# Weighted sums with the support stationary: one float32r matmul in place of four bf16 matmuls in a two-layer graph kernel

## The chip, the cores and the metric

The kernel runs on one core of a Trainium2 chip. The metric is the device time of one execution in microseconds (us); lower is better. The engines are TensorE (PE; its weight loads are PEld), VectorE (DVE), ScalarE (ACT), GpSimd (POOL) and SyncE (SP), which here issues nearly all DMAs. SBUF is the core's memory, PSUM the one that TensorE writes to.

## The reference

Two graph layers with residuals over 2048 nodes of 64 features; `adj` is a sparse 2048 x 2048 matrix of zeros and ones.

```python
# layer 0
support = x @ weight
mask = (adj != 0)
rank = cumsum(mask, axis=1); deg = rank[:, -1:]
k = minimum(deg, 100.0)
pos = rank - (deg - k)
w = mask * where(pos > 0, 0.5 ** (k - pos), 0.0)
x = layernorm(x + w @ support + bias)
# layer 1
deg = clip(sum(adj, axis=1, keepdims=True) + 1, 1, None)
h = (adj @ x + x) / deg
z = relu(concatenate([x, h], axis=1) @ W + b)
x = layernorm(x + z / maximum(norm(z), 1e-12))
```

The weight of an edge is a power of two whose exponent is the number of ones to its right in its row.

## The kernel before, in words

The rows of `adj` (2048) stand in four quarters q = 0..3 of 512 rows, its columns in 16 blocks b of 128. It is loaded in 16 units of 1 MB (`stage`, a ring of 8), one for a quarter and four column blocks. SP issues all loads in a fixed order, u0 to u15. A unit is turned so that columns stand on partitions (`adjT`): TensorE transposes it in two groups of eight 128 x 128 pieces into a bank of `tmp` (L837) and DVE copies that out (L533). The last four units (u12 to u15) are turned by DMA instead: DVE packs such a unit to bf16 in four casts (`pack`, L488), and SP issues a DMA transpose (L239).

Layer 0 runs as two chains, c = 0 (quarters 0, then 2) and c = 1 (quarters 1, then 3), each 32 steps long, from the last column block to the first. Step n of a chain does three things.

- `count`: two 512-column matmuls (L856 with `rest`, L858 with `suffix`) add to a PSUM bank `cnt[:, c]` so that it holds, for every edge of this block, the bit pattern of its power of two.
- `weights` (ACT, L324): a Relu that writes these as int16, which read as bf16 are the weights `wts`. The next `count` of this chain adds to the same bank and waits for it, so that a chain can't step faster than one round trip PE - ACT - PE.
- `weigh`: for each 128 of the 512 rows a matmul with the weights stationary and `sup` moving (L869, four of 192 columns) adds to `acc`. `sup` is the support in three bf16 parts, side by side.

A hand-written loop over ticks orders all engines. In tick t TensorE does `count(0, t)`, `weigh(0, t - 3)`, what belongs to index m = t + 2 (transposes of a group of `adj`, x1T, yu), `count(1, t - 5)` and `weigh(1, t - 8)`. DVE runs over the same m in its own order: parts of `finish_layer0`, the copy of the group, then `pack` where PACKS says so (m = 21 to 24). Every queue is in order, so what DVE has in front of a copy holds the `count` that reads it.

`finish_layer0(q, part)` turns the sums of a quarter into `x1`: part 0 adds the three parts of the sum (a reduction from `acc`, L455), part 1 adds `xs` (L458), part 2 takes statistics (L438), part 3 centres (L464), part 4 scales (four small operations L443 to L447, then L469). x1 is transposed (L879) and multiplied by W (L888, "yu"), and parts 6 and 7 split the result into three bf16 parts `ysp`. Layer 1's aggregation (L900) and its elementwise end follow.

Of the kernel before, what the change touches and what calls it, by code (L numbers as in the profile page):

```python
# [44 lines left out]
F32 = mybir.dt.float32  # L45
BF16 = mybir.dt.bfloat16
# [3 lines left out]
def build(nc, x, adj, w0, b0, w1, b1, out):  # L50
    with ExitStack() as ctx:
# [25 lines left out]
        ident32 = sb("ident32", [P, P], F32)  # L77
        wd0 = sb("wd0", [P, 2, D], F32)
# [22 lines left out]

        agg = [acc[:, 0:RT, :], cnt[:, :, :].rearrange("p b (h n) -> p (b h) n", h=2), acc[:, RT:2 * RT, :],
# [8 lines left out]
        wd_zeroed = sem("wd_zeroed")  # L111
        zeroed = sem("zeroed")
# [8 lines left out]
        sup_left = sem("sup_left")  # L121
        sup_mid = sem("sup_mid")
# [4 lines left out]
        w_ready = [sem(f"w_ready{i}") for i in range(2)]  # L127
        w_used = [sem(f"w_used{i}") for i in range(2)]
# [46 lines left out]
        for m in range(TICKS):  # L175
# [11 lines left out]
        fills += [("x1T", 2), ("yu", 2), ("x1T", 3), ("yu", 3)]  # L187
# [59 lines left out]
        def _(pool):  # L247
# [18 lines left out]
            select(rest, ALU.not_equal, -float(EXP1 * (NEIGH + 1))).then_inc(consts, 1)  # L266
            nc.gpsimd.memset(power[:, :], -0.5).then_inc(power_set, 1)
# [754 lines left out]
```

## Time and profile before

| | |
|---|---|
| median of 3 runs | 111.45 us (111.05 to 112.16) |
| the profiled execution | 110.99 us, of which the span from first to last instruction is 109.2 us |
| busy: PE, PEld, DVE, ACT, POOL | 91.9, 73.7, 61.3, 58.0, 18.8 us |
| chain that ended last | PE 72%, DVE 13%, DMA 4%, ACT 4% |
| mean granted TensorE clock | 0.975 |

Times are counted from the first instruction. A row of the groups gives busy time and the mean of one instruction, which for a matmul holds its latency: back to back they start much closer. What a matmul costs in a stream is read from the chain that ended last, where its row holds only the time by which it moved the chain. The rows of a DMA's issue and of its landing are in two views: landing is counted from the start of the issue.

### The profile page before, as it was taken

The numbers are of one execution on the slowest core, as the hardware profiler recorded it, in microseconds if no ns is written. First come the engines' busy times: TensorE is split into PE (matmuls) and PEld (weight loads), VectorE is DVE, ScalarE is ACT, GpSimd is POOL, SyncE is SP. The second block draws the span as 40 slices with busy tenths as digits, with TensorE's granted clock in tenths as the row PEclk, the third lists the DMA queues.
The fourth block names the chain that finished last, engine by engine and source line by source line (L and its number), as shares of the span: only waits on it lengthen the run. The fifth ranks groups of instructions, "written<-read, shape, count | busy, mean of one in ns | idle before, by whom it ended". The sixth has DMA issues, their size and how long they took to land.

```text
span 109.2 us, 2379 instructions
## 1 busy us (share of the span) xinstructions
PE 91.9 (84%) x876; PEld 73.7 (67%) x876; DVE 61.3 (56%) x186; ACT 58.0 (53%) x126; POOL 18.8 (17%) x44
## 2 busy tenths in 40 slices
PE   0349299999999999999999999999999999996000
PEld 0248068777777777777676676678988999995000
DVE  1003527564525247899998402226378339999991
ACT  0602644396665656666648886633214208479640
POOL 6200000000000142200074200000000000367870
PEclk9999999999999999999999999999999999999955
DMA  2999999799999999999799910000000000000224
GB/s 61 297 300 349 373 388 369 252 393 388 385 388 388 384 389 385 386 378 202 169 213 212 115 28 0 6 0 0 0 6 0 0 0 0 6 0 0 48 53 94
DMA packets 22314, 20.23 MB, mean 185 GB/s; under 512 B 13600, under 2 KB 14624, under 8 KB 22304
## 3 DMA queue, kind: packets, MB, share of 16 engines
q1 hardware_dynamic: 22144, 20.06, 61.2%
q8 instruction: 7, 0.11, 0.4%
q10 hardware_dynamic: 160, 0.03, 0.1%
q14 instruction: 3, 0.02, 0.1%
HBM read 17.47 MB, written 0.52 MB: 165 GB/s over the span
## 4 chain that ended last, share of the span: by engine, by line
PE 72%; DVE 13%; DMA 4%; ACT 4%; issue 3%; SPq 1%; DVEq 0%
PE acc L869 18%; PE cnt L856 13%; PE cnt L858 12%; PE tmp L837 10%; PE acc L900 7%; PE cnt L900 5%; DMA stage<-in_adj_dram 4%; PE tmp L888 3%; DVE stats L438 3%; DVE t L571 3%; ACT wts L324 2%; PE acc L914 2%; DVE t L582 1%; PE tmp L879 1%; PE tmp L914 1%
## 5 line engine op out<-in xcount | busy, mean ns | idle before, releaser
L324 ACT ACTIVATE wts<-cnt 128x512 int16<-128x512 f32 x64 | 37.8, 597 | 23.1 <-PE cnt L858 22.8
L869 PEld LDWEIGHTS acc<-sup,wts 128*128 128x128 bf16 x256 | 22.9, 98 | 13.5
L869 PE MATMUL acc<-sup,wts 128*128 128x192 bf16 x256 | 31.2, 246 | 0.0
L533 DVE COPY adjT<-tmp 128x1024 bf16<-128x1024 bf16 x24 | 16.5, 688 | 20.9 <-PE tmp L837 20.9
L856 PE MATMUL cnt<-adjT,rest 128*128 128x512 bf16 x60 | 22.8, 380 | 2.3 <-ACT wts L324 2.2
L858 PE MATMUL cnt<-adjT,suffix 128*128 128x512 bf16 x64 | 24.5, 383 | 0.0
L837 PE MATMUL tmp<-ident,stage 128*128 128x128 bf16 x192 | 15.5, 227 | 1.9 <-DMA stage<-in_adj_dram 1.9
L275 POOL TENSOR_TENSOR adjT<-adjT,ident 128x128 bf16<-128x128 bf16 x16 | 7.3, 487 | 49.9 <-PE cnt L858 49.9
L837 PEld LDWEIGHTS tmp<-ident,stage 128*128 128x128 bf16 x192 | 13.1, 102 | 3.0 <-issue 2.5
L900 PE MATMUL acc<-ysp,adjT 128*128 128x194 bf16 x128 | 12.4, 247 | 0.0
L900 PEld LDWEIGHTS acc<-ysp,adjT 128*128 128x128 bf16 x128 | 11.0, 98 | 0.2
L279 POOL TENSOR_TENSOR small<-square,power 128x4 f32<-128x4 f32 (+1 forms) x4 | 4.2, 1056 | 34.5 <-DVE square L603 34.5
L856 PEld LDWEIGHTS cnt<-adjT,rest 128*128 128x128 bf16 x60 | 5.8, 97 | 4.5 <-ACT wts L324 3.7
L374 ACT ACTIVATE u<-u,degree 128x64 f32<-128x64 f32 x16 | 4.4, 337 | 4.9 <-DVE degree L567 4.8
L455 DVE TENSOR_REDUCE t<-acc 128x256 f32<-128x768 f32 x4 | 3.8, 954 | 5.4 <-PE acc L869 5.4
L858 PEld LDWEIGHTS cnt<-adjT,suffix 128*128 128x128 bf16 x64 | 6.3, 99 | 0.4
L900 PE MATMUL cnt<-ysp,adjT 128*128 128x194 bf16 x64 | 6.4, 247 | 0.0
L474 DVE TENSOR_TENSOR left<-tmp,ysp 128x256 f32<-128x256 f32 x4 | 1.7, 419 | 7.5 <-ACT ysp L335 7.5
L438 DVE BATCH_NORM_STATS2 stats<-t 128x6 f32<-128x128 f32 x23 | 5.7, 285 | 0.1
L488 DVE CAST nat<-stage 128x512 bf16<-128x512 f32 x16 | 5.7, 417 | 0.0
L900 PEld LDWEIGHTS cnt<-ysp,adjT 128*128 128x128 bf16 x64 | 5.5, 98 | 0.2
L900 PE MATMUL tmp<-ysp,adjT 128*128 128x194 bf16 x64 | 5.6, 247 | 0.0
(98 smaller groups left out, 83.8 us busy)
## 6 DMA issues: line engine op xcount, KB each, us to landing
stage<-in_adj_dram SPq DMA_DIRECT2D x15, 1024.0 KB, 14.0
stage<-in_adj_dram SPq DMA_DIRECT2D x4, 256.0 KB, 4.4
xs<-in_x_dram SPq DMA_DIRECT2D x2, 256.0 KB, 5.7
out_dram<-xs SPq DMA_DIRECT2D x3, 128.0 KB, 2.0
out_dram<-xs SPq DMA_DIRECT2D x2, 64.0 KB, 1.7
wd<-in_L_gnn_W_dram SPq DMA_DIRECT2D x4, 16.0 KB, 8.3
adjT<-nat SPq DMA_TRANSPOSE x4, 5.4
wd<-in_L_gnn_weight_dram ACTq DMA_DIRECT2D x2, 16.0 KB, 4.0
```

The lines of the kernel that those rows point to most:

```text
L275: nc.gpsimd.tensor_tensor(d, d, ident16[:, :], ALU.add).then_inc(diag_ready, 1)
L279: nc.gpsimd.tensor_tensor(small[:, 3, batch(k)], square[:, batch(k)], power[:, 0:size(k)], ALU.pow).then_inc(norm_ready[k], 1)
L324: nc.scalar.activation(wts[:, c, n % WRING, :].bitcast(I16), cnt[:, c, :], ACT.Relu).then_inc(w_ready[c], 1)
L374: nc.scalar.activation(u1[:, t, :], u1[:, t, :], ACT.Copy, scale=degree[:, t:t + 1]).then_inc(weighted[k], 1)
L438: yield nc.vector.bn_stats(stats[:, k, t:t + 2, :].rearrange("p s c -> p (s c)"), data[:, t:t + 2, :].rearrange("p t d -> p d t"))
L488: nc.vector.tensor_copy(nat[:, i, r, :], stage[:, u % RING, r, :]).then_inc(nat_ready, 1)
L533: nc.vector.tensor_copy(adjT[:, q, bp // 2, :, bp % 2 * 2:bp % 2 * 2 + 2, :], bank.bitcast(BF16).rearrange("p (r k n) -> p r k n", r=RT, k ...
L837: last = nc.tensor.transpose(bank[:, (2 * r + k) * P:(2 * r + k + 1) * P], halves[:, r, 2 * j0 + 1:2 * (j0 + P):2], ident16[:, :])
L856: nc.tensor.matmul(cnt[:, c, :], rest[:, :], block_of(q, b + 1), start=False, stop=False, skip_group_check=True)
L858: nc.tensor.matmul(cnt[:, c, :], suffix[:, :], block_of(q, b), start=(b == NB - 1), stop=True, skip_group_check=True).then_inc(cnt_done[c], 1)
L869: last = nc.tensor.matmul(acc[:, c * RT + r, 0:PD], wts[:, c, n % WRING, r * P:(r + 1) * P], sup[:, b, :], start=(b == NB - 1 and r % 2 == ...
L900: last = nc.tensor.matmul(agg[g][:, r, 0:PD + 2], adjT[:, g, b // QB, r, b % QB, :], ysp[:, b, 0:PD + 2], start=first, stop=(b == NB - 1), ...
```

## The change

`weigh` becomes one matmul: `sup` (128 columns, now two float32r parts of 64) is stationary, the 512 weights of the step stream past it as float32r, and the result is the transposed sum [128 = 2 parts x 64, 512 rows] in one bank `accT[q]`. ACT writes the weights as before, now to `w16`; a new POOL copy (`widen`) makes float32r of them. When a quarter ends, ACT copies the bank to SBUF (`copy_sums`) and TensorE multiplies each 128 rows of it by `fold`, two stacked identities (`fold_sums`, four float32 matmuls of 64 columns), which transposes back and adds the parts. Part 0 on DVE goes; parts 1 to 7 and what follows them come one or two ticks later. The split of the support needs one DVE operation where it needed two and an ACT copy.

In the head, ten matmuls on zeros (`warm`) stand before and after the first transposes, DVE and no longer ACT copies the first xT, and `ORDER` swaps m = 5 and 6. The operations on the diagonal (POOL, L275) are placed in the tick loop. The casts of `pack` stay at m = 21 to 24.

```diff
-WHEN = {0: (0, 1, 2), 1: (3,), 2: (4,), 6: (6,), 7: (7,)}
-WRING = 4
+WHEN = {2: (1, 2), 3: (3,), 4: (4,), 7: (6,), 8: (7,)}
+WRING = 3
+SRING = 2
+ORDER = (0, 1, 2, 3, 4, 6, 5) + tuple(range(7, TICKS))
+WARM = (6, 4)
+DIAG_AT = (16, 18, 25, 27)
+COPIED = (NB - 1 + LAG, NB - 1 + LAG + BEHIND, STEPS - 1 + LAG)
...
+            def widen(c, n):
+                pool.wait_ge(w_ready[c], n + 1)
+                if n >= WRING:
+                    pool.wait_ge(w_used[c], n - WRING + 1)
+                nc.gpsimd.tensor_copy(wts[:, c, n % WRING, :], w16[:, c, n % SRING, :]).then_inc(w_cast[c], 1)
...
+            def copy_sums(q):
+                act.wait_ge(w_used[q % 2], (q // 2 + 1) * NB)
+                if q >= 2:
+                    act.wait_ge(tmp_full, number[("sum", q - 1)] + 1)
+                nc.scalar.copy(sums[:, min(q, 1), :], accT[q]).then_inc(acc_read, 1)
...
-                if part == 0:
-                    dve.wait_ge(w_used[c], (q // 2 + 1) * NB)
-                    sums = acc[:, c * RT:(c + 1) * RT, 0:PD].rearrange("p t (k d) -> p t d k", k=PARTS)
-                    nc.vector.reduce_sum(t0[:, v, :], sums, AX_X).then_inc(acc_read, 1)
...
-                for r in range(RT):
-                    last = nc.tensor.matmul(acc[:, c * RT + r, 0:PD], wts[:, c, n % WRING, r * P:(r + 1) * P],
-                                            sup[:, b, :], start=(b == NB - 1 and r % 2 == 0), stop=(b == 0),
-                                            skip_group_check=True)
-                last.then_inc(w_used[c], 1)
+                nc.tensor.matmul(accT[q], sup[:, b, :], wts[:, c, n % WRING, :], start=(b == NB - 1), stop=(b == 0),
+                                 skip_group_check=True).then_inc(w_used[c], 1)
+
+            def fold_sums(q):
+                bank = tmp_bank(("sum", q))
+                pe.wait_ge(acc_read, q + 1)
                 for r in range(RT):
+                    last = nc.tensor.matmul(bank[:, r * D:(r + 1) * D], sums[:, min(q, 1), r * P:(r + 1) * P], fold[:, :],
+                                            start=True, stop=True)
+                last.then_inc(tmp_full, 1)
```

TensorE's row around ticks 24 to 26, before: first the transposes of x1 of quarter 0, then count(1, 18) and so on; the third pair of counts is count(1, 19), behind the transposes of group m = 26.

```order
L879 MATMUL tmp<-ident,x 128x128 x2
L856 MATMUL cnt<-adjT,rest 128x512
L858 MATMUL cnt<-adjT,suffix 128x512
L869 MATMUL acc<-sup,wts 128x192 x4
L856 MATMUL cnt<-adjT,rest 128x512
L858 MATMUL cnt<-adjT,suffix 128x512
L869 MATMUL acc<-sup,wts 128x192 x4
L888 MATMUL tmp<-wd,x1T 128x256 x2
L837 MATMUL tmp<-ident,stage 128x128 x8
L856 MATMUL cnt<-adjT,rest 128x512
L858 MATMUL cnt<-adjT,suffix 128x512
L869 MATMUL acc<-sup,wts 128x192 x4
```

The same stretch now, from count(0, 24); L860 are the transposes of `adj`, L879 and L881 `count`, L889 `weigh`, L905 x1T, L914 yu.

```order
L879 MATMUL cnt<-adjT,rest 128x512
L881 MATMUL cnt<-adjT,suffix 128x512
L889 MATMUL acc<-wts,sup 128x512
L905 MATMUL tmp<-ident,x 128x128 x2
L860 MATMUL tmp<-ident,stage 128x128 x8
L879 MATMUL cnt<-adjT,rest 128x512
L881 MATMUL cnt<-adjT,suffix 128x512
L889 MATMUL acc<-wts,sup 128x512
L879 MATMUL cnt<-adjT,rest 128x512
L881 MATMUL cnt<-adjT,suffix 128x512
L889 MATMUL acc<-wts,sup 128x512
L914 MATMUL tmp<-wd,x1T 128x256 x2
```

Four matmuls have become one, and x1T and yu of the quarter each stand one tick later.

DVE's row from the first pack (m = 21) to the copy of the group m = 24 and the last pack, before (L443 to L469 are part 4).

```order
L488 CAST nat<-stage 128x512 x4
L443 RECIPROCAL small<-root 128x4
L444 SCALAR_TENSOR_TENSOR small<-small 128x4
L445 SCALAR_TENSOR_TENSOR small<-stats,small 128x4
L447 SCALAR_TENSOR_TENSOR small<-small 128x4
L469 TENSOR_TENSOR x<-t,small 128x256
L533 COPY adjT<-tmp 128x4x256
L488 CAST nat<-stage 128x512 x4
L533 COPY adjT<-tmp 128x4x256
L488 CAST nat<-stage 128x512 x4
L533 COPY adjT<-tmp 128x4x256
L488 CAST nat<-stage 128x512 x4
```

And now, from the second pack (m = 22) to the copy of the group m = 26 (L517 is the cast of a pack, L557 the copy of a group).

```order
L517 CAST nat<-stage 128x512 x4
L493 SCALAR_TENSOR_TENSOR t<-stats,t 128x256
L557 COPY adjT<-tmp 128x4x256
L517 CAST nat<-stage 128x512 x4
L475 RECIPROCAL small<-root 128x4
L476 SCALAR_TENSOR_TENSOR small<-small 128x4
L477 SCALAR_TENSOR_TENSOR small<-stats,small 128x4
L479 SCALAR_TENSOR_TENSOR small<-small 128x4
L498 TENSOR_TENSOR x<-t,small 128x256
L557 COPY adjT<-tmp 128x4x256
L517 CAST nat<-stage 128x512 x4
L557 COPY adjT<-tmp 128x4x256
```

Part 4 now stands between the third pack and the copy of the group m = 24, where nothing stood.

TensorE's row at the end of chain 1, before: the last three `weigh` with aggregation (L900) between them, then x1T and yu of quarter 2.

```order
L900 MATMUL acc<-ysp,adjT 128x194 x8
L869 MATMUL acc<-sup,wts 128x192 x4
L900 MATMUL acc<-ysp,adjT 128x194 x8
L869 MATMUL acc<-sup,wts 128x192 x4
L900 MATMUL acc<-ysp,adjT 128x194 x8
L869 MATMUL acc<-sup,wts 128x192 x4
L879 MATMUL tmp<-ident,x 128x128 x2
L900 MATMUL cnt<-ysp,adjT 128x194 x8
L888 MATMUL tmp<-wd,x1T 128x256 x2
```

And now (L926 is aggregation, L896 `fold_sums`).

```order
L926 MATMUL acc<-ysp,adjT 128x194 x8
L896 MATMUL tmp<-fold,u 128x64 x4
L889 MATMUL acc<-wts,sup 128x512
L926 MATMUL acc<-ysp,adjT 128x194 x8
L889 MATMUL acc<-wts,sup 128x512
L926 MATMUL acc<-ysp,adjT 128x194 x8
L889 MATMUL acc<-wts,sup 128x512
L905 MATMUL tmp<-ident,x 128x128 x2
L926 MATMUL cnt<-ysp,adjT 128x194 x8
L896 MATMUL tmp<-fold,u 128x64 x4
L914 MATMUL tmp<-wd,x1T 128x256 x2
```

The sum of quarter 2, which DVE took when chain 0 had ended, is now made on TensorE, three `weigh` and two aggregations ahead of x1T.

## Rows read from the trace of the kernel before

**Rows 1.** The page: the span in 40 slices of 2.73 us

```profile
PE   0349299999999999999999999999999999996000
...
DVE  1003527564525247899998402226378339999991
...
PEclk9999999999999999999999999999999999999955
...
GB/s 61 297 300 349 373 388 369 252 393 388 385 388 388 384 389 385 386 378 202 169 213 212 115 28 0 6 0 0 0 6 0 0 0 0 6 0 0 48 53 94
```

**Rows 2.** The chain that ended last: start us, us moved; one full tick

```profile
32.28 0.45 PE tmp L837 x8
32.73 0.22 PE cnt L856
...
33.16 0.33 PE acc L869 x4
...
34.25 0.45 PE tmp L837 x8
```

**Rows 3.** The same chain: the head, and float32 matmuls later

```profile
6.93 1.01 PE tmp L837 x8
7.94 1.83 PE acc L914 x8
9.79 0.61 ACT sup L310
10.42 0.70 DVE left L497
11.15 0.62 ACT sup L313
11.76 0.51 ACT wts L324
12.32 0.39 PE cnt L856
...
20.20 0.92 PE tmp L914 x8
...
64.55 0.22 PE tmp L879 x2
...
66.30 0.89 PE tmp L888 x4
```

**Rows 4.** SP's timeline: issues of the loads u13, u14, u15

```profile
32.76 1.11 SPq L236 DMA_DIRECT2D stage<-in_adj_dram  x1
...
34.73 3.76 SPq L236 DMA_DIRECT2D stage<-in_adj_dram  x1
...
40.43 0.76 SPq L236 DMA_DIRECT2D stage<-in_adj_dram  x1
```

**Rows 5.** DMA view over each issue of Rows 4: KB, us from issue to landing

```profile
stage<-in_adj_dram SPq DMA_DIRECT2D x1, 1024.0 KB, 15.2
...
stage<-in_adj_dram SPq DMA_DIRECT2D x1, 1024.0 KB, 15.9
...
stage<-in_adj_dram SPq DMA_DIRECT2D x1, 1024.0 KB, 12.8
```

**Rows 6.** Timeline, ticks 21 to 26: start us, us, what

```profile
48.77 0.17 DVE L443 RECIPROCAL small<-root 128x4 f32<-128x4 f32 x1
...
49.56 0.42 DVE L469 TENSOR_TENSOR x<-t,small 128x256 f32<-128x256 f32 x1
...
52.44 1.42 DVE L488 CAST nat<-stage 128x512 bf16<-128x512 f32 x4
...
53.78 0.68 DVE L533 COPY adjT<-tmp 128x1024 bf16<-128x1024 bf16 x1
...
54.61 0.38 PE L856 MATMUL cnt<-adjT,rest 128*128 128x512 bf16 x1
```

**Rows 7.** Timeline, ends of the chains

```profile
68.55 0.38 PE L856 MATMUL cnt<-adjT,rest 128*128 128x512 bf16 x1
...
69.86 0.39 PE L856 MATMUL cnt<-adjT,rest 128*128 128x512 bf16 x1
...
79.82 0.96 DVE L455 TENSOR_REDUCE t<-acc 128x256 f32<-128x768 f32 x1 [1.25 <-PE acc L869]
...
83.06 0.42 DVE L469 TENSOR_TENSOR x<-t,small 128x256 f32<-128x256 f32 x1
```

**Rows 8.** Timeline: POOL

```profile
2.51 0.29 POOL L254 TENSOR_SCALAR_AFFINE_SELECT rest<-rest 128x128 bf16<-128x128 bf16 x1
...
37.95 1.20 POOL L275 TENSOR_TENSOR adjT<-adjT,ident 128x128 bf16<-128x128 bf16 x3 [34.23 <-PE cnt L858]
...
55.28 2.14 POOL L275 TENSOR_TENSOR adjT<-adjT,ident 128x128 bf16<-128x128 bf16 x4 [10.82 <-PE cnt L858]
```

**Rows 9.** Groups by line, engine and form: busy us, mean ns of one

```profile
L250 POOL MEMSET suffix<- 128x128 bf16 x1 | 0.2, 205 | 0.0
L267 POOL MEMSET power<- 128x4 f32 x1 | 0.1, 102 | 0.0
```

More of the change, by code:

```diff
@@ L45 @@
 F32 = mybir.dt.float32
+F32R = mybir.dt.float32r
 BF16 = mybir.dt.bfloat16
@@ L127, in build @@
         w_ready = [sem(f"w_ready{i}") for i in range(2)]
+        w_cast = [sem(f"w_cast{i}") for i in range(2)]
         w_used = [sem(f"w_used{i}") for i in range(2)]
@@ L174, in build @@
         fills = []
-        for m in range(TICKS):
+        for m in ORDER:
             if m == XT0:
@@ L275, in _ @@
                     nc.gpsimd.tensor_tensor(d, d, ident16[:, :], ALU.add).then_inc(diag_ready, 1)
+            for tick in range(TICKS):
+                if tick < STEPS:
+                    widen(0, tick)
+                if tick >= BEHIND:
+                    widen(1, tick - BEHIND)
+                for q in range(Q):
+                    if tick == DIAG_AT[q]:
+                        diagonal(q)
             def norm_power(k):
@@ L339, in y_middle @@
                 act.wait_ge(y_left, q + 1)
-                nc.scalar.copy(ysp[:, rows(q), D:2 * D], left32[:, rows(q), :]).then_inc(y_mid, 1)
+                nc.scalar.copy(ysp[:, rows(q), D:2 * D], t0[:, rows(q), :]).then_inc(y_mid, 1)
             for tick in range(TICKS):
@@ L361, in _ @@
                     weights(1, tick - BEHIND)
+                for q in range(3):
+                    if tick == COPIED[q]:
+                        copy_sums(q)
             spread_root0(2)
+            copy_sums(3)
             copy_x1T(2)
@@ L535, in _ @@
                         tmp_read[number[("adj", q, bp)] % 2], 1)
-                for i in range(TURNED):
-                    if m == PACKS[i]:
-                        pack(i)
-            for q, part in ((2, 0), (2, 1), (2, 2), (2, 3), (2, 4), (3, 0), (3, 1), (3, 2), (3, 3), (3, 4), (2, 6), (2, 7),
+                for i, r in PIECES.get(m, ()):
+                    pack(i, r)
+            for q, part in ((2, 1), (2, 2), (2, 3), (2, 4), (3, 1), (3, 2), (3, 3), (3, 4), (2, 6), (2, 7),
                             (3, 6), (3, 7)):
@@ L922, in acc_bank, with warm @@
                 return lambda k: acc[:, t + k // 2, (k % 2) * P:(k % 2 + 1) * P]
+            def warm(n):
+                zeros = w16[:, 0, 0, :]
+                for _ in range(n):
+                    nc.tensor.matmul(cnt[:, 0, :], zeros[:, 0:P], zeros, start=True, stop=True,
+                                     skip_group_check=True)
+            pe.wait_ge(warm_set, 1)
+            warm(WARM[0])
             pe.wait_ge(ident32_ready, 1)
             transpose_x(1, acc_bank(2)).then_inc(xT_done, 1)
+            warm(WARM[1])
             pe.wait_ge(consts, 1)
```

110 lines of the change are left out of this document (54 added, 56 removed).

## The prediction

> **What bounds the kernel now.** I read the 40 slices first [rows 1]: TensorE is at nine tenths from slice 5 to 36, DVE is full only in slices 17 to 21 and at the end, and the DMA engines move a flat 385 GB/s up to slice 17. So I looked at one tick in the chain that ended last [rows 2]: 1.97 us, which is four count matmuls at 0.22 (0.87), two weighs at 0.33 and eight transposes at 0.45. TensorE has no gap there. That makes the change look good: it takes 0.11 off each of 64 weighs. But a tick needs data too. A load's landing is its issue plus its time to land [rows 4, 5]: u13 lands at 32.76 + 15.2 = 48.0, u14 at 34.73 + 15.9 = 50.6, u15 at 40.43 + 12.8 = 53.2. They are 2.6 us apart, which is 1 MB at the rate of [rows 1], so they come at the DMA engines' pace, whatever TensorE does. DVE packs u14 at 52.44 and was at the next copy at 53.78, and count(0, 24), which reads that copy, starts at 54.61 [rows 6]. The kernel before is therefore within 2 us of a second bound: the loads, passed on by DVE's queue. How far the change can pull everything ahead of it is the question.
>
> **The head.** Before: transposes 6.93, support 1.83, three operations ACT, DVE, ACT, the first weights, and count(0, 1) at 12.32 [rows 3]. The eight support records took 1.83 there and 0.92 at 20.20 [rows 3]: half speed is the 1.2 GHz level (the PEclk row prints 9 there all the same [rows 1]), after an engine that had been idle up to the first data. With ten matmuls ahead I expect the 2.4 GHz level: transposes 0.45, support 0.92, ACT 0.6 twice (the middle part of the split no longer stands before the first weights), so count(0, 1) at 6.93 + 0.45 + 0.92 + 0.17 + 0.60 + 0.60 = 9.7, a gain of 2.6. If the clock stays low it is 1.3. Then chain 0 alone runs at the round trip of 1.3 (68.55 to 69.86 in [rows 7]), which the change doesn't touch, and waits for the next units on the way; I carry 2.0 of the gain to tick 10.
>
> **The price of a weigh.** No row shows a float32r matmul. Bounds: as the bf16 one of 512 columns, 0.22 [rows 2]; as a float32 transpose, which at 0.22 for two of 128 columns takes twice the time of a bf16 one, 0.43 [rows 3]; as a full float32 matmul, 0.89 for two of 256 columns and so 0.89 for one of 512 [rows 3]. I take 0.22: the operands are split into two short parts so that one pass is enough. The weight load is hidden as it is in the float32 rows. So a weigh costs 0.11 less. The Trainium skill (FP8 and Floating Point Precision, TensorE Precision Notes) says that float32 in reduced precision is read and truncated, while true float32 takes 4 passes; by it the price is one pass, 0.22, and no run here shows it yet.
>
> **fold_sums** is four float32 matmuls, eight records. Eight records of 128 columns took 0.92 [rows 3]; 64 columns stream in half of that, 0.46, but each record still loads 128 columns of weights. I take 0.88, with 0.45 as the other end. Four of them: +3.5 us on TensorE against 64 x 0.11 = 7.0 saved. ACT's copies (0.6 each) lie beside TensorE except for some tenths.
>
> **widen on POOL.** From memsets, a POOL operation costs 0.10 fixed and (205 - 102)/124 = 0.83 ns an element [rows 9]; a select with one input took 0.29 for 128 elements, so 1.5 ns an element [rows 8]; a two-input one follows the last after 0.40, so about 1.3 us for 512 elements [rows 8]. The copy is then 0.53, 0.88 or 1.3 us. I take 0.55, since it computes nothing and so is nearest to the memset, and starts every 0.5 us: two a tick, 1.0 of 1.3 to 1.75 us, three ticks ahead of their use. It costs nothing while that holds. The Trainium skill (GPSIMD Engine Reference, Engine selection) calls one-input operations roughly line-rate; the select in [rows 8] is well above that. The same page (Elementwise — side-by-side cycle accounting) also has 769 ns measured for 512 elements at 1.8 cycles; by that figure the copy lies between my two and the time some 1.5 us above the forecast.
>
> **How far the gain gets.** On its own TensorE would reach count(0, 24) at 54.61 - 2.0 (head) - 14 x 0.23 (ticks 10 to 23) + 0.9 (fold of quarter 0) = 50.3. But DVE's queue holds its input. u14 lands at 50.63 [rows 4, 5]; the pack takes 1.42 [rows 6]; part 4, which the change puts behind that pack, 49.56 + 0.42 - 48.77 = 1.2 [rows 6]; then the copy, 0.69. That is 53.95, and TensorE waits for it, 3.6 us in all. So count(0, 24) gains only 54.61 - 53.95 = **0.66**. Behind it the last pack (u15, landed at 53.2) and the copy of group 26 end at 56.1, in time.
>
> **From count(0, 24) to count(1, 26)** (before: 54.61 to 68.55 [rows 6, 7]) there are 15 weighs, -15 x 0.11 = -1.7; the fold of quarter 1, +0.9; x1T of quarter 0, which stood before this stretch, +0.2. Sum **-0.6**, and count(1, 26) starts 1.3 earlier.
>
> **From there to the end of aggregation** (the next two count steps run at the 1.3 round trip, so weighs give nothing): eight weighs, -0.9; two folds, +1.8. And a new wait: before, DVE reduced quarter 2 as soon as chain 0 had ended. Now its fold stands behind the aggregation of tick 36. From the end of a fold to x1 it is 0.2 + what follows the reduction in [rows 7], 83.06 + 0.42 - 79.82 - 0.96 = 2.7, so 2.9; TensorE has three weighs and two aggregations (0.68 each) in front of x1T, 2.0. It waits 0.9 to 1.0. For quarter 3 the work in front (3.0) nearly covers it. Sum **+1.9**. What follows (17.9 us) is not changed.
>
> **Sum**: -0.66 - 0.6 + 1.9 = +0.65 on the profiled execution of 110.99, so 111.6. That execution lies 0.46 below the median of the runs, so the forecast is **112.1 us**, against 111.45.
>
> **Rivals.**
> First, the gain survives (faster). The loads, or what DVE does about them, don't hold TensorE at tick 24; 3.6 us of waiting fall away and the time is 112.1 - 3.6 = 108.5. For it: the rate of [rows 1] dips to 252 in slice 7, so the loads aren't at their limit throughout. Against: eight slices after it are flat. Chance 0.18.
>
> Second, POOL is the bound (slower). At the select's price copies start every 0.82 us. In ticks 25 to 31, of some 1.3 us and with 2.2 of fold and yu, TensorE asks for 14 copies (11.5) and eight diagonal operations (3.2 or more) within 11.3 us; the lead of three ticks covers about 1.0 to 1.5 of the 3.4 missing. Some 2.5 more: 114.6. It decides from 0.65 us a copy. The diagonal operations also took 2.14 for four where DVE was packing, against 1.20 for three without [rows 8], and the packs are in this stretch. The Trainium skill (GPSIMD Engine Reference, Key points) says that POOL shares its SBUF interfaces with DVE; by that rule it is the copies beside the packs that grow, and these rows agree. Chance 0.18. (At the two-input price POOL would need 9.7 + 64 x 1.3 + 7 = 100 for the last weigh, which was at 79: over 20 us more.)
>
> Third, float32r streams at half rate, 0.43 (slower). Then each weigh costs 0.10 more: count(0, 24) at 54.61 - 2.0 + 2.8 + 0.9 = 56.3 (+1.7; the loads don't bind), +1.5 + 1.1 to count(1, 26), and 1.2 + 1.8 + 0.7 behind it: +8.0, so 119.5. At the full float32 price it would be 64 x 0.56 = 36 more. Chance 0.10.
>
> Fourth, the warm-up doesn't raise the clock. It costs nothing in the end, since TensorE waits for loads later anyway: 112.1 too. Chance 0.04.
>
> **Numbers.** Forecast 0.50 (its own range 110.2 to 113.4: folds at 0.45 give -1.7, waits on ACT and a clock that falls in a gap of 2.7 us up to +1.3). A measurement of this kernel can tell about 1% from no change, so the marks are 110.3 and 112.6. Forecast: 0.03 faster, 0.34 same, 0.13 slower; faster 0.18; POOL and half rate 0.28 slower; the fourth 0.04 same. Together 0.21, 0.38, 0.41. The range leaves out the half rate and part of the first rival: 109.0 to 116.0.
>
> **What the profile after should show.** A weigh moves the chain by 0.22, a full tick is 1.74 or less wherever there is no wait, a fold moves it by 0.9, a POOL cast lasts 0.5 to 0.6, and count(0, 1) starts near 9.7. u14 and u15 land within half a microsecond of 50.6 and 53.2. DVE stands still before packs, the first time until about 45, and TensorE waits 2 us or more for the copy of group 24 near 54. x1T of quarter 2 is waited for by about 1 us. I'm wrong if the loads land earlier, if DVE has no idle time before its packs, or if ACT or TensorE waits for POOL.

## The result, and the profile after

The changed kernel takes **117.44 us** (median of 4 runs, 116.13 to 118.8) where the kernel before took 111.81 (median of 4, 111.05 to 112.3): a ratio of 1.042, 95% interval 1.030 to 1.054. The forecast was 112.1, in a range of 109.0 to 116.0. (Some executions of every kernel here are disturbed and 1 to 3% longer; the ratios leave them out but the medians don't, and two of the profiled executions are among them, that of the changed kernel, with 118.18 beside 116.13 and 116.70, and that of experiment 6.) The profiled execution took 118.18, with a span of 116.5 against 109.2.

The page of the changed kernel, its slices now 2.91 us long, beside [rows 1]:

```profile
PE   5996989987999999499299998999979999997000
...
DVE  2224654636424423999941652310446556999981
...
POOL 6304444666666899644424899944200000067770
PEclk9999999999999999986959999999999999999755
```

TensorE has holes at slices 16 and 19, DVE is full from slice 16 to 19, POOL is busy for 50% of the span where it was for 17%, and the granted clock falls twice. Where that comes from is seen in DVE's timeline (start us, us, what), beside [rows 6]:

```profile
46.40 2.83 DVE L517 CAST nat<-stage 128x512 bf16<-128x512 f32 x4 [1.88 <-DMA stage<-in_adj_dram]
...
50.59 1.84 DVE L517 CAST nat<-stage 128x512 bf16<-128x512 f32 x4
52.34 0.82 DVE L493 SCALAR_TENSOR_TENSOR t<-stats,t 128x256 f32<-128x256 f32 x1
...
53.81 1.83 DVE L517 CAST nat<-stage 128x512 bf16<-128x512 f32 x4
55.56 0.16 DVE L475 RECIPROCAL small<-root 128x4 f32<-128x4 f32 x1
55.76 0.41 DVE L476 SCALAR_TENSOR_TENSOR small<-small 128x4 f32<-128x4 f32 x1
...
57.23 0.68 DVE L557 COPY adjT<-tmp 128x1024 bf16<-128x1024 bf16 x1
57.84 1.42 DVE L517 CAST nat<-stage 128x512 bf16<-128x512 f32 x4
```

A pack of four casts took 1.42 before [rows 6] and takes 1.42, 1.83, 1.84 or 2.83 now; L493 takes 0.82, and 0.42 where nothing is beside it. The copy out of `tmp` (L557) is as it was. POOL's timeline shows what lay beside the long ones:

```profile
47.53 1.41 POOL L289 CAST wts<-w 128x512 fp32r<-128x512 bf16 x2 [0.42 <-ACT w L349]
51.22 1.67 POOL L289 CAST wts<-w 128x512 fp32r<-128x512 bf16 x2 [2.27 <-ACT w L349]
54.26 0.77 POOL L289 CAST wts<-w 128x512 fp32r<-128x512 bf16 x1 [1.36 <-ACT w L349]
```

From 56.8 to 59.8 POOL waits for ACT, and the pack at 57.84 has its 1.42 back. TensorE's timeline has the two waits that follow:

```profile
49.70 0.61 PE L860 MATMUL tmp<-ident,stage 128*128 128x128 bf16 x8 [1.94 <-DVE t L486]
...
58.06 0.58 PE L879 MATMUL cnt<-adjT,rest 128*128 128x512 bf16 x1 [2.31 <-DVE adjT L557]
```

The windows view (TensorE busy, granted clock, DMA share, GB/s) shows the clock behind them:

```profile
48.00:50.00 2.00, 0.30 (x6) 1.00 0.81 302
...
52.00:54.00 2.00, 2.00 (x11) 0.50 0.14 36
...
56.00:58.00 2.00, 0.00 (x0) 1.00 1.24 97
58.00:60.00 2.00, 1.94 (x8) 0.53 1.25 274
```

After each nearly empty window the clock is at its 1.2 GHz level (0.50 of 2.4) for some 3.4 us, and it is back after that.

I cut every span at four marks that the kernels share: the starts of count(0,21), count(0,24) and count(1,26), and the end of the span. All in us, each from the profiled execution. The first two rows are the kernels compared; the others are told below. The last two columns rest on a span known to 0.1 us.

| kernel | count(0,21) | from 21 to 24 | to count(1,26) | to the end | span |
|---|---|---|---|---|---|
| before | 48.87 | 5.74 | 13.94 | 40.65 | 109.2 |
| changed | 46.91 | 11.15 | 15.82 | 42.62 | 116.5 |
| changed, waits filled | 46.24 | 11.05 | 14.15 | 42.56 | 114.0 |
| changed, no warm-up | 47.85 | 10.72 | 14.15 | 42.58 | 115.3 |
| changed, packs later | 46.74 | 8.51 | 14.17 | 42.58 | 112.0 |
| the same, five casts on ACT | 46.67 | 7.77 | 15.81 | 42.55 | 112.8 |
| changed, idle casts | 46.95 | 10.71 | 14.48 | 43.66 | 115.8 |
| changed, no cast | 46.86 | 6.77 | 14.25 | 43.62 | 111.5 |
| changed, no cast, ring 4 | 46.00 | 7.04 | 13.54 | 42.62 | 109.2 |
| the same, packs later | 47.57 | 6.23 | 13.54 | 42.56 | 109.9 |
| before, all idle casts | 49.63 | 9.59 | 13.93 | 40.65 | 113.8 |
| before, ten at the packs | 49.47 | 7.28 | 14.34 | 40.71 | 111.8 |
| before, the other 54 | 50.29 | 7.12 | 13.92 | 40.67 | 112.0 |
| before, changed head | 50.38 | 5.74 | 13.93 | 40.85 | 110.9 |

The change lost 7.3 us of span: -2.0 up to count(0,21), **+5.4 in the three ticks from 21 to 24**, +1.9 to count(1,26), +1.9 to +2.0 behind it. The 5.4 don't hang on one execution: the changed kernel with its waits filled and the one without warm-up, which have the same casts and the same order, took 11.05 and 10.72 for these ticks.

Of the stretch behind it, the chain that ended last says one thing more. From 64.5 to 71.7 it runs through POOL:

```profile
65.11 1.19 POOL adjT L295 x3
...
71.04 0.56 POOL wts L289
...
71.69 0.61 ACT w L349
```

There the casts and the diagonal's operations follow each other, and ACT, which writes into a ring of two, waits 0.97 us for a cast. In all ACT waited 3.5 us for POOL, in five waits, two of them in the head and three between 70.7 and 77.1.

### The profile page after: what moved, and what is told of

The parts are those of the page before. It is cut to its first block, busy times and chain, and to the rows that moved or that the text cites. A ratio compares the mean times of both kernels' runs of the same rounds, so it can differ in the third digit from the quotient of the medians.

```text
span 116.5 us, 2207 instructions
## 1 busy us (share of the span) xinstructions
PE 96.4 (83%) x726; PEld 65.6 (56%) x726; DVE 61.6 (53%) x182; ACT 58.2 (50%) x127; POOL 58.0 (50%) x109
## 4 chain that ended last, share of the span: by engine, by line
DMA 25%; PE 25%; DVE 23%; SPq 12%; issue 6%; POOL 4%; ACT 2%; DVEq 0%; ACTq 0%
DMA stage<-in_adj_dram 25%; SPq L248 6%; DVE nat L517 6%; PE acc L926 5%; PE cnt L926 5%; DVE stats L470 3%; PE tmp L914 3%; PE cnt L879 3%; PE cnt L881 3%; DVE t L594 2%; POOL wts L289 2%; PE acc L889 2%; POOL adjT L295 2%; ACT w L349 2%; SPq L228 2%
## 5 line engine op out<-in xcount | busy, mean ns | idle before, releaser
L289 POOL CAST wts<-w 128x512 fp32r<-128x512 bf16 x64 | 40.1, 645 | 32.5 <-ACT w L349 31.9
L349 ACT ACTIVATE w<-cnt 128x512 int16<-128x512 f32 x64 | 37.8, 597 | 30.1 <-PE cnt L881 25.0
L889 PE MATMUL acc<-wts,sup 128*128 128x512 f32 x64 | 37.4, 591 | 0.0
L879 PE MATMUL cnt<-adjT,rest 128*128 128x512 bf16 x60 | 24.0, 401 | 4.5 <-DVE adjT L557 2.3
L557 DVE COPY adjT<-tmp 128x1024 bf16<-128x1024 bf16 x24 | 16.5, 689 | 20.1 <-PE tmp L860 20.1
L881 PE MATMUL cnt<-adjT,suffix 128*128 128x512 bf16 x64 | 25.3, 395 | 0.0
L860 PE MATMUL tmp<-ident,stage 128*128 128x128 bf16 x192 | 15.7, 228 | 4.0 <-DMA stage<-in_adj_dram 2.0
L860 PEld LDWEIGHTS tmp<-ident,stage 128*128 128x128 bf16 x192 | 12.0, 103 | 10.7 <-issue 6.4
L889 PEld LDWEIGHTS acc<-wts,sup 128*128 128x128 f32 x64 | 12.8, 199 | 7.3 <-issue 1.1
L879 PEld LDWEIGHTS cnt<-adjT,rest 128*128 128x128 bf16 x60 | 6.0, 100 | 14.3 <-issue 7.9
L926 PE MATMUL acc<-ysp,adjT 128*128 128x194 bf16 x128 | 12.2, 247 | 0.0
L926 PEld LDWEIGHTS acc<-ysp,adjT 128*128 128x128 bf16 x128 | 10.6, 98 | 1.0 <-issue 0.3
L517 DVE CAST nat<-stage 128x512 bf16<-128x512 f32 x16 | 7.9, 556 | 1.9 <-DMA stage<-in_adj_dram 1.9
L486 DVE TENSOR_TENSOR t<-tmp,xs 128x256 f32<-128x256 f32 x4 | 1.7, 420 | 10.2 <-PE tmp L896 10.2
L881 PEld LDWEIGHTS cnt<-adjT,suffix 128*128 128x128 bf16 x64 | 6.5, 101 | 0.8 <-issue 0.3
L926 PE MATMUL cnt<-ysp,adjT 128*128 128x194 bf16 x64 | 6.3, 247 | 0.0
L503 DVE TENSOR_TENSOR t<-tmp,ysp 128x256 f32<-128x256 f32 x4 | 1.7, 422 | 7.8 <-ACT ysp L366 7.8
L926 PEld LDWEIGHTS cnt<-ysp,adjT 128*128 128x128 bf16 x64 | 5.3, 98 | 0.7 <-issue 0.5
```

The lines of the kernel that those rows point to most:

```text
L289: nc.gpsimd.tensor_copy(wts[:, c, n % WRING, :], w16[:, c, n % SRING, :]).then_inc(w_cast[c], 1)
L349: nc.scalar.activation(w16[:, c, n % SRING, :].bitcast(I16), cnt[:, c, :], ACT.Relu).then_inc(w_ready[c], 1)
L517: nc.vector.tensor_copy(nat[:, i, r, :], stage[:, u % RING, r, :]).then_inc(nat_ready, 1)
L557: nc.vector.tensor_copy(adjT[:, q, bp // 2, :, bp % 2 * 2:bp % 2 * 2 + 2, :], bank.bitcast(BF16).rearrange("p (r k n) -> p r k n", r=RT, k ...
L860: last = nc.tensor.transpose(bank[:, (2 * r + k) * P:(2 * r + k + 1) * P], halves[:, r, 2 * j0 + 1:2 * (j0 + P):2], ident16[:, :])
L879: nc.tensor.matmul(cnt[:, c, :], rest[:, :], block_of(q, b + 1), start=False, stop=False, skip_group_check=True)
```

## The experiments

**1. No cast.** ScalarE writes float32r itself. The weights are then the counts as numbers, so that this kernel and those of 2, 5 and 13 do the same work but do not compute the reference:

```diff
-  nc.scalar.activation(w16[:, c, n % SRING, :].bitcast(I16), cnt[:, c, :], ACT.Relu).then_inc(w_ready[c], 1)
+  nc.scalar.activation(wts[:, c, n % WRING, :], cnt[:, c, :], ACT.Relu).then_inc(w_ready[c], 1)
```

> The changed kernel without POOL's casts: ScalarE writes the counts themselves, as numbers, into the float32r weights (so the weights' values are other ones, and the 64 POOL casts and w16 are left out); everything else, float32r weigh, fold, head, order and the shorter ring, is the change's. Theory A (POOL's casts slow DVE's SBUF-to-SBUF operations, and the late count(0,24) and the slow clock follow from that): the packs fall from a mean of 0.56 us back to 0.42, the first of 2.83 us to 1.4, count(0,24) comes near my 53.95 instead of 58.06, no stretch of TensorE at 1.2 GHz between 50 and 62 us, count(1,26) at 67 to 68.5, total 109 to 112. Theory B (the order of the pieces, the loads and the float32r weigh are at fault, not the casts): count(0,24) stays at 57 or later and the total at 115 to 117.5. Theory C (only that the cast stands on the path from a count to its weigh, POOL's throughput): count(0,24) stays at 57 to 58, and only the stretch from there to count(1,26) shrinks from 15.8 to about 13.5, total about 115.

Measured: 114.25 us (113.52 to 114.72), 1.026 of before (1.015 to 1.038). count(0,24) came at 53.63, where I had forecast 53.95 with no price on the cast. The packs are back:

```profile
44.97 1.43 DVE L513 CAST nat<-stage 128x512 bf16<-128x512 f32 x4 [0.60 <-DMA stage<-in_adj_dram]
...
47.77 1.42 DVE L513 CAST nat<-stage 128x512 bf16<-128x512 f32 x4
49.11 0.42 DVE L489 SCALAR_TENSOR_TENSOR t<-stats,t 128x256 f32<-128x256 f32 x1
```

So without the casts 4.4 of the 11.15 us from 21 to 24 are gone, and the clock doesn't fall. But the total was 2 us above theory A's range, and the waits show one reason: "ACT wts L345 <- PE acc L885: 21.3, 33, 1.6". Without `w16` between, a ring of 3 and a lag of 3 tie ScalarE to the weigh; the changed kernel's ScalarE has no such wait in its list, so it is this experiment's own (see 5).

**2. Idle casts in the changed kernel.** Experiment 1 and, on POOL, a cast that nobody waits for, at the signal of the real one:

```diff
+            def idle_cast(c, n):
+                pool.wait_ge(w_ready[c], n + 1)
...
+                nc.gpsimd.tensor_copy(zout[:, :], w16[:, 0, 0, :]).then_inc(z_done, 1)
```

> As the kernel without casts (weights are the counts as numbers), with 64 POOL casts of the same shape from a constant tile to a tile that nobody reads, each released by the same signal as the real ones were; no weigh waits for them (the diagonal's eight operations still stand behind them). Theory A: nearly as slow as the changed kernel up to count(0,24): packs' mean 0.52 to 0.58, count(0,24) 57 to 58.5, total 114 to 117, so 4 us or more above the kernel without casts. Theory C (the path through POOL): within 1 us of the kernel without casts. Difference between this one and the changed kernel: what the cast costs as a link of the path, which I put at 1 to 2 us.

Measured: 119.41 us (117.63 to 120.77), 1.062 (1.042 to 1.081): by the two ratios some 4 us above experiment 1, and the stretch from 21 to 24 at 10.71 against 6.77. The casts needn't hand over anything to cost this. The last sentence of the expectation can't be judged here: this kernel isn't faster than the changed one, but its ScalarE waits for a weigh (25.6 us in 35 waits), as in experiment 1 and not in the changed kernel, so their difference isn't the price of the cast as a link of the path.

**3. Idle casts in the kernel before**, on a constant tile:

```diff
+                nc.gpsimd.tensor_copy(zout[:, :], z16[:, :]).then_inc(z_done, 1)
...
+                    if tick == (16, 18, 25, 27)[q]:
+                        diagonal(q)
```

> The kernel before, complete, with 64 idle POOL casts of a constant bf16 tile to a float32r tile added, released by the same signals, and the diagonal's operations put between them at the same ticks as in the changed kernel. Theory A: the casts alone make the kernel before slower: packs from 0.417 to 0.5 or more, count(0,24) from 54.6 to 56.5 to 58, total from 111.5 to 113.5 to 116. Theories B and C: no change, within 0.5 us of the kernel before.

Measured: 116.43 us (115.83 to 119.28), 1.046 (1.028 to 1.064), as large as the change's whole loss and somewhat above the expected 113.5 to 116. In its trace the packs' group reads

```profile
L513 DVE CAST nat<-stage 128x512 bf16<-128x512 f32 x16 | 8.9, 618 | 0.0
```

618 ns a cast (the changed kernel: 556; experiment 1: 434). Except for 0.8 ahead of count(0,21), where the granted clock was 0.50 from 14 to 17 us, the loss lies wholly between 21 and 24 (+3.85); the two later stretches are those of the kernel before to 0.01. The float32r weigh, the folds and the new order aren't in this kernel at all.

**4. The waits filled.** 18 matmuls of a zero tile keep TensorE busy where it waits:

```diff
+                if m == 24:
+                    fill(8)
...
+                if tick == 24:
+                    fill(10)
```

> The changed kernel, complete, with 18 matmuls of a zero tile added into an accumulator (0.22 us each, 4 us in all): 8 ahead of the transposes for tick 24 and 10 ahead of count(0,24), where TensorE idled 1.9 and 2.3 us. They tell what the fallen clock costs. Theory A with the clock as a follower: count(0,24) stays late, at 57 to 58, but the 3.3 us after it at 1.2 GHz go back to 2.4: total 1.5 to 2.5 us below the changed kernel, about 115.5. If the clock alone were the cause (theory D): total 112.5 or less. If the clock costs nothing here (other engines bound those ticks): 117 to 118.

Measured: 118.43 us (115.76 to 118.88), no gain on 117.44 that the spread would show. The profiled execution has no window under full clock between 44 and 74 us, and its stretch to count(1,26) took 14.15 against 15.82. So the fallen clock cost 1.7 us in the profiled execution of the changed kernel. Theory D is out: no execution came below 115.76. In the medians the clock is not seen. The changed kernel without warm-up had 14.15 in that stretch too: the second fall of the clock isn't in every execution. The first fall cost nothing that shows (11.05 here against 11.15), since TensorE waits for DVE there at either clock.

**5. No cast, and a ring of 4.**

```diff
-WRING = 3
+WRING = 4
```

> The kernel without casts (weights are the counts as numbers), its ring of weights 4 deep instead of 3, as the kernel before has it. In the kernel without casts and with a ring of 3, ScalarE waited 21.3 us in 33 waits for a weigh, count(0,24) came at 53.63 and the rest took 57.9 us from there (before: 54.6). Theory: the ring of 3 with a lag of 3 ties ScalarE to the weigh; with 4 the waits for a weigh vanish, the stretch count(0,24) to count(1,26) falls from 14.25 to 13.3 to 13.9 and the end comes 1 to 2 us earlier: 112 to 113. If the float32r weigh and the folds cost the rest: still 114.

The waits of ScalarE for a weigh are gone, the stretch to count(1,26) is 13.54 (13.3 to 13.9 expected) and the rest 42.62 (43.62 with the ring of 3, 40.65 before). The profiled execution took 111.16, but the median of 6 was 113.23 (111.16 to 114.07), 1.019 (1.007 to 1.031), beside 1.026 for experiment 1: the stretches show what the ring cost there, the totals are too scattered to.

**6. The head alone.** The kernel before with ten warm-up matmuls and the copy of xT on VectorE:

```diff
+            pe.wait_ge(warm_set, 1)
+            warm(6)
             pe.wait_ge(ident32_ready, 1)
             transpose_x(1, acc_bank(2)).then_inc(xT_done, 1)
+            warm(4)
```

> The kernel before, complete, with the head of the changed one alone: six and four warm-up matmuls of a zero tile, and the copy of the first transposed x on VectorE instead of ScalarE. By my prediction's terms: count(0,1) from 12.32 to about 9.9 (gain 2.4), of which at count(0,24) only 0.3 to 0.7 is left, since the loads bound it there: total 0.3 to 0.7 us below before, 111.2 to 111.7 beside 112.0. Rival: the head's gain survives: 109.5 to 110. Other rival: it is lost entirely, 112.

Measured: 112.56 us (110.83 to 114.2, 10 runs), 1.001 (0.993 to 1.009). The second rival holds for the time: lost entirely. In the profiled execution count(0,1) started at 10.49, 1.8 earlier, but ticks 3 and 4 took 3.3 and 3.0 us where those of the kernel before took 1.3 and 1.7, and count(0,21) came at 50.38, later than before. Windows and timeline show why:

```profile
13.00:15.00 2.00, 1.75 (x8) 0.50 1.05 390
```

```profile
15.52 1.03 PE L839 MATMUL tmp<-ident,stage 128*128 128x128 bf16 x8 [0.77 <-DMA stage<-in_adj_dram]
```

TensorE, which had waited 1.28 and 0.69 us for ACT before counts 1 and 2, was at the 1.2 GHz level from 12.3 to 19.1, so that a tick's work of 1.2 to 1.7 us took nearly twice as long, and one load was awaited for 0.8 besides. So in this execution the clock took most of the gain back, and a load the rest. Whether the same keeps the ratio at 1.001 isn't shown; the bound by the loads at tick 24 could do it too.

**7 and 8. The idle casts split in two.** Experiment 3 with ten casts in ticks 20 to 24, and with the other 54:

```diff
-                if tick < STEPS:
+                if tick < STEPS and 20 <= tick <= 24:
                     widen(0, tick)
```

> The kernel before, complete, with idle POOL casts of a constant tile only in ticks 20 to 24, beside VectorE's packs: 10 of the 64 of the run with all of them (which took 116.43 beside 112.1). Theory A: nearly the whole loss comes from these ten: packs' mean 0.55 to 0.62, count(0,24) at 57 to 59, total +3 to +4.3. Rival (the loss comes from POOL's load as a whole, through ScalarE's or the diagonal's waits): +0.7 or less.

> The kernel before, complete, with idle POOL casts in all ticks but 20 to 24 (54 of the 64). Theory A: packs' mean near 0.42, count(0,24) at 54.6 to 55.5, total 0 to +0.8 beside before, since VectorE's other work in those ticks has idle time around it. Rival: +3 to +4.3.

Measured: 113.25 us (112.9 to 114.77), 1.016 (1.005 to 1.027) with the ten; 114.02 (113.53 to 114.68), 1.024 (1.014 to 1.034) with the others. Both expectations for theory A missed: the ten are not nearly all, and the 54 are not free. The stretch from 21 to 24 grows by 1.5 us with the ten and by 1.4 with the 54, together 2.9 of the 3.85 with all. POOL's and DVE's timelines of the kernel with the 54:

```profile
45.63 3.09 POOL L283 CAST zout<-z 128x512 fp32r<-128x512 bf16 x4
48.69 2.13 POOL L291 TENSOR_TENSOR adjT<-adjT,ident 128x128 bf16<-128x128 bf16 x4
50.77 1.55 POOL L283 CAST zout<-z 128x512 fp32r<-128x512 bf16 x2
```

```profile
48.89 2.21 DVE L513 CAST nat<-stage 128x512 bf16<-128x512 f32 x4
...
51.22 0.36 DVE L469 SCALAR_TENSOR_TENSOR small<-small 128x4 f32<-128x4 f32 x1
```

POOL is behind by then, and its diagonal operations and late casts fall on the first pack. The other 1.4 us stood before count(0,21), and they are the clock's: up to 18 us a count matmul of that execution took 0.61 to 0.63, as at the 1.2 GHz level, where the kernel before had 0.38 to 0.39 from 12.32 on. (The windows view prints a clock of 1.00 there, as in the head of the kernel before.) Experiment 6 lost 1.5 there without any cast.

**9. VectorE's operations beside a cast, by themselves.** A kernel of its own: eight of each kind while POOL rests, then the same eight beside a row of casts, each of which waits for the end of the one before it.

> A kernel of its own, which computes nothing of the reference and stores x back: VectorE does six kinds of this kernel's operations, 8 of each, first while GpSimd rests and then beside an unbroken row of POOL casts (bf16 to float32r, 128x512, SBUF to SBUF); POOL casts 8 times alone between. From the traces so far: the pack's cast (SBUF to SBUF, 0.36 us alone), the operation of two SBUF inputs (0.41) and the small one of 128x4 (0.16) stretch to about one POOL cast each (0.6 to 0.75 us) when beside it; the copy out of PSUM (0.69), the sum with an operand in PSUM (0.41) and the statistics do not change. POOL's cast: 0.6 us alone, 0.7 to 1.2 beside. Rival: all of VectorE's operations stretch by the same share, as they would by a shared memory rate.

Groups by line and form (busy us, mean ns of one); the lines from 122 to 139 are alone, those from 152 to 169 beside POOL's L111:

```profile
L111 POOL CAST zout<-z 128x512 fp32r<-128x512 bf16 x64 | 40.8, 638 | 4.0
L158 DVE SCALAR_TENSOR_TENSOR p<-a,b 128x256 f32<-128x256 f32 x8 | 6.0, 821 | 0.0
L152 DVE CAST o<-a 128x512 bf16<-128x512 f32 x8 | 5.7, 778 | 6.1 <-POOL y L107 6.1
L105 POOL CAST zout<-z 128x512 fp32r<-128x512 bf16 x8 | 4.9, 616 | 17.2 <-DVE b L148 16.7
L125 DVE COPY c<-bank 128x1024 bf16<-128x1024 bf16 x8 | 4.9, 678 | 0.0
L155 DVE COPY c<-bank 128x1024 bf16<-128x1024 bf16 x8 | 4.9, 674 | 0.0
L122 DVE CAST o<-a 128x512 bf16<-128x512 f32 x8 | 2.8, 418 | 0.0
L128 DVE SCALAR_TENSOR_TENSOR p<-a,b 128x256 f32<-128x256 f32 x8 | 2.8, 414 | 0.0
L132 DVE TENSOR_TENSOR q<-bank,b 128x256 f32<-128x256 f32 x8 | 2.7, 411 | 0.0
L162 DVE TENSOR_TENSOR q<-bank,b 128x256 f32<-128x256 f32 x8 | 2.7, 407 | 0.0
L165 DVE BATCH_NORM_STATS2 stats<-a 128x6 f32<-128x128 f32 x8 | 1.6, 273 | 0.0
L135 DVE BATCH_NORM_STATS2 stats<-a 128x6 f32<-128x128 f32 x8 | 1.6, 275 | 0.0
L169 DVE SCALAR_TENSOR_TENSOR small<-a,b 128x4 f32<-128x4 f32 x8 | 1.4, 237 | 0.0
L139 DVE SCALAR_TENSOR_TENSOR small<-a,b 128x4 f32<-128x4 f32 x8 | 0.7, 153 | 0.0
```

The pack's cast doubles (418 to 778), so does the operation on two SBUF tiles (414 to 821), the small one goes from 153 to 237. The copy out of PSUM, the sum with an operand in PSUM and the statistics don't move by more than 4 ns. So the rival of one shared rate for all of VectorE's operations is out: they take turns. Beside them POOL starts a cast every 0.75 us, and every 0.68 alone or beside the other three kinds; DVE's casts and its operations on two tiles start every 0.75 as well, one for each cast of POOL. Of the eight small ones two were held (0.42 and 0.57), and the six others, three at a time behind a held one, ran at their 0.15, so that their mean grew less than expected. The Trainium skill (GPSIMD Engine Reference, Key points) puts the contention on VectorE's instructions "in a 2-port perf mode or with two SBUF inputs"; by that rule these three kinds suffer and the other three don't, and the run agrees on all six. My prediction had only the first half of that sentence.

One POOL operation is not the most that one DVE operation can wait. In the changed kernel no cast waits for the one before, and casts that are due start 0.56 us apart, each before the last has ended. Where such a row is unbroken, DVE's cast is held to its end. From the kernel of experiment 11 (the first line gives the shortest, median and longest cast of DVE in ns; experiment 4 has one of 2273):

```profile
L517 DVE CAST nat<-stage x16: 408/414/2230, 46.1 to 59.4; 128x512 bf16<-128x512 f32 x16
```

```profile
44.78 1.58 POOL L295 TENSOR_TENSOR adjT<-adjT,ident 128x128 bf16<-128x128 bf16 x4
46.31 1.72 POOL L289 CAST wts<-w 128x512 fp32r<-128x512 bf16 x3
```

DVE's cast started at 46.08, when its load was there, and ended at 48.31, behind the last of these three.

**10. The packs one place later.**

```diff
-PIECES = {21: ((0, 0), (0, 1), (0, 2), (0, 3)), 22: ...
+PIECES = {22: ((0, 0), (0, 1), (0, 2), (0, 3)), 23: ..., 24: ..., 26: ...}
```

> The changed kernel, complete, with VectorE's packs one place later in its order (22, 23, 24, 26 instead of 21 to 24), so that the first no longer stands ahead of a part of layer 0 and an adjT copy while its load is awaited. If the order is what costs (theory B): count(0,24) 2 us earlier than 58.06 and the total 115.5 or less. By theory A the packs cost their stretched 1.8 us each wherever POOL casts beside them: within 1 us of the changed kernel, 116.5 to 118.5.

Measured: 115.08 us (113.72 to 117.44), 1.019 (1.008 to 1.029), outside theory A's range on the good side and within theory B's, as is count(0,24) at 55.25, 2.8 earlier. The casts are as slow as ever (group mean 572 ns), but only 8.51 us pass from 21 to 24:

```profile
46.70 0.67 DVE L557 COPY adjT<-tmp 128x1024 bf16<-128x1024 bf16 x1
47.29 2.66 DVE L517 CAST nat<-stage 128x512 bf16<-128x512 f32 x4
49.87 0.82 DVE L493 SCALAR_TENSOR_TENSOR t<-stats,t 128x256 f32<-128x256 f32 x1
50.73 0.69 DVE L557 COPY adjT<-tmp 128x1024 bf16<-128x1024 bf16 x1
```

In the changed kernel the first pack stands ahead of part 1 and of this copy, waits 1.9 for its load and then takes 2.8, and TensorE's transposes wait for what is queued behind it (49.99 against 46.70 for the copy). So the order has a share, some 2.6 us of the 5.4, by making the stretched pack wait in front. Without casts the two places differ by 0.8 there (7.04 in 5, 6.23 in 13).

**11. No warm-up.** `WARM = (0, 0)` in the changed kernel.

> The changed kernel, complete, without its ten warm-up matmuls, which is the largest piece of my term for the head (a gain of 2.6 us at count(0,1), 2.0 from tick 10). In the traces the loads that end ticks 4 and 5 take the head's gain away again in the kernel before with the changed head. If that holds here too: count(0,1) 0.8 to 1.5 us later than 9.59, count(0,21) within 0.6 us of 46.91, total the same within 0.7 us, 116.7 to 118.2. Rival: the loss is carried through, +1 to +1.5.

Measured: 118.38 us (117.14 to 120.68), 1.059 (1.044 to 1.074), 0.9 above the changed kernel's median, with intervals that overlap. count(0,1) is 1.5 later, count(0,21) 0.9. Here, unlike in the kernel before, most of the head's gain reaches tick 21. Whether it reaches the end stays open.

**12. Packs later, and five casts on ScalarE.**

```diff
+                nc.scalar.copy(wts[:, 0, n % WRING, :], w16[:, 0, n % SRING, :]).then_inc(w_cast[0], 1)
```

> The changed kernel, complete, with the packs one place later and, in ticks 20 to 24, chain 0's five casts done by ScalarE (w16 to the float32r weights) instead of POOL. With the packs later it took 115.08 beside 111.8. If the stretched packs are what is left in ticks 20 to 24 (their mean 572 ns, 4 times 4 of them): mean down to 0.48 to 0.52, count(0,24) from 55.25 to 54 to 54.6, total 113.5 to 114.5. If ScalarE's extra 0.6 us a tick becomes the bound there (it has 1.2 us of work in a tick of 1.8): 115 or more.

Measured: 115.14 us (113.75 to 116.3, 6 runs), 1.029 (1.018 to 1.040). The casts' mean fell to 495 ns and count(0,24) came at 54.44, both as expected, but the next stretch took 15.81 for 14.17. It isn't shown that ScalarE was the bound there: the granted clock was 0.50 from 56 to 58 (low from some 55.7 to 59), after TensorE had waited 2.83 us for count(0,24), and 1.6 us is what the same fall cost in the changed kernel. By the totals (1.029 against 1.019 with intervals that overlap) the five casts moved nothing.

**13. No cast, ring of 4, packs later.** Experiments 5 and 10 together.

> The kernel without casts and a ring of 4 (weights are the counts as numbers), with the packs one place later. Its span with the old places was 109.2 in the profile (before: 109.2) and its median 113.2 beside 112.6. If the place of the packs matters only beside the casts: within 0.5 us of that, 111 to 113, no better than before. If the place costs by itself (the load awaited ahead of the adjT copy): count(0,24) from 53.04 to 51.5 to 52.3 and the total 1 to 1.5 us lower, faster than before.

Measured: 111.34 us (110.34 to 113.06, 12 runs), 0.998 (0.993 to 1.002). This is the change with its casts taken away: no different from the kernel before. Its -0.8 at count(0,24), -0.4 to count(1,26) and +1.9 behind make +0.7 of span, where the prediction's sum is +0.65. Whether the place of the packs matters without casts stays open: the medians of 5 and 13 are 1.9 us apart, but the two shortest executions of 5 (111.16 and 112.02) are level with 13, and so are the spans (109.2 and 109.9).

No complete version beat the kernel before. The whole advantage in reach, by 13, is within what can be measured. A complete kernel with a ring of 4 wasn't run.

## Why the prediction was wrong

**The step that failed** is the one on `widen`, "It costs nothing while that holds", together with the pack that "takes 1.42" in "How far the gain gets". I asked whether POOL could keep up with its casts, and it nearly does: 645 ns for one, where I took 0.55, and ACT waited 3.5 us for it in all. I didn't ask what the casts do to the engine beside them. Each takes DVE's turn at SBUF, and DVE is the engine on which count(0,24) waits. In the changed kernel three packs (2.83, 1.84, 1.83 for 1.42 each: 2.2), L493 (0.4) and two small operations (0.25 and 0.3) make 3.2 us of the 4.1 by which count(0,24) missed 53.95. From 46.40, when the first pack had its load, to that copy DVE had no gap, so these 3.2 us counted in full. The other 0.9 is as much as the loads were late in that execution: u14 was issued at 34.46 and took 17.2, so landed at 51.7, where 50.6 was forecast and experiment 1 had 50.3. What made them late isn't shown.

- *The head*: count(0,1) forecast 9.7, was 9.59; carry to tick 10 forecast 2.0, was 2.35. Right in this kernel. The kernel before with this head lost its gain, in the profiled execution mostly to the clock (experiment 6).
- *From tick 10 on*: by the sum's own terms (0.23 a tick for two weighs, 0.9 for a fold) count(0,21) had to come at 45.2; it came at 46.91. A full tick took 1.80 where 1.74 was forecast, and ticks 10 and 11 waited for loads (0.36 and 0.73 us). This step was off by 1.7 us. That it didn't count was luck: count(0,24) waits for DVE's queue at either time.
- *A weigh*: 0.22 forecast; its rows in the chain read 0.23 to 0.26 at full clock. Right to 0.01 in most.

```profile
30.01 0.23 PE acc L889
...
82.29 0.88 PE tmp L896 x8
...
86.01 0.41 PE tmp L905 x2
```

- *fold_sums*: 0.88 forecast, 0.88 measured. Right.
- *Up to count(0,24)*: -0.66 forecast, +3.45 measured. Without casts, -0.98 (experiment 1), -1.57 (5) and -0.81 (13). The bound by loads and DVE's queue was read rightly: in experiment 1 the pack of u14 starts at 50.31, as its load lands, and count(0,24) comes at 53.63 for 53.95. It is also why DVE's slowing counted in full.
- *To count(1,26)*: -0.6 forecast, +1.88 measured; 1.7 of it is the clock in the profiled execution, and POOL on the chain, its casts and the diagonal's operations, makes some 0.6 (14.15 in 4, 13.54 in 5). Without casts it is -0.4.
- *Behind it*: +1.9 forecast, +1.9 to +2.0 measured (TensorE waited 0.69 for x1T of quarter 2, where 0.9 to 1.0 was forecast), and the same in every kernel with the folds but those with ScalarE tied to the weigh (1 and 2).
- *The rivals.* The first (108.5), the third (float32r at half rate) and the fourth fell. The second, POOL as the bound at 114.6, had the side, and the fact that it needs. What it describes did happen in ticks 27 to 30, where the chain runs through POOL, but it is worth 0.6 us and not 2.5. The large loss was another: I had POOL's operations growing in ticks 25 to 31, and it was DVE's in ticks 21 to 24. It had 0.18, and the range of 116.0 rested on it.

So with the casts taken out the span comes to 0.0 (experiment 5) and +0.7 (13) against before, where the sum says +0.65: the other terms hold to less than 1 us together. With the casts in, the term that the sum put at nothing was worth 4 to 5 us: 3.2 on DVE and 0.6 on POOL in the profiled execution, 0.998 in 13 against 1.042 for the change, and 1.046 for the casts alone in the kernel before. That is the error; the fallen clock comes on top in the profiled execution.

## What to carry to other kernels

Work that is moved to an idle GpSimd is not free when VectorE works beside it: list VectorE's operations by where their operands are, and add the length of at least one GpSimd operation to each SBUF-to-SBUF cast and each operation on two SBUF tiles that falls beside it (where GpSimd's operations follow each other without a wait, it was up to four, 2.23 us for a cast of 0.42); those that read PSUM lost nothing in experiment 9. Price it where VectorE's queue is what the next engine waits for, and test it before the whole change is written, by adding idle operations of the same shape to the old kernel (experiment 3 gave 1.046, the change 1.042). And an item in a queue that awaits a load should stand behind what is due already, above all when it may grow.

## What the runs showed that I had not expected

- VectorE and GpSimd take turns by whole operations: even one of 128 x 4 elements, 153 ns alone, took 0.35 to 0.58 us in the kernels where a cast was running. GpSimd pays little in experiment 9 (a start every 0.75 against 0.68 us).
- A row of GpSimd operations without waits between them doesn't let VectorE in: a cast of 0.42 us took 2.23 (experiment 11) and 2.27 us (4).
- A float32r matmul of 512 columns moves the chain by 0.23 us, nearly the same as bf16 (0.22), and its weight load of 190 to 199 ns stays hidden.
- After TensorE had waited 1.9 to 2.8 us, 3.3 to 3.4 us at the 1.2 GHz level followed in the changed kernel (twice) and in experiment 12, and none in experiment 10 after 2.86 us or in 11 after 2.11. A fall behind count(0,24) cost 1.6 to 1.7 us in each of the two executions that had one, and nothing that shows in the medians.
- The head's gain of 1.8 us was gone by tick 5 in the kernel before, in an execution in which TensorE was at the 1.2 GHz level from 12.3 to 19.1 us.
